# An attention kernel in which PE issues each odd step's scores before the pair's value products, instead of behind them

## The chip, the cores and the metric

One Trainium2 chip, one of its cores. The metric is the device time of one execution in microseconds. The engines are PE (matrix products and transposes), DVE (vector), ACT (scalar and activation), POOL (GpSimd) and SP (it issues DMA here). Each takes its own instructions in the order in which the program lists them, and semaphores tie the engines together.

## The reference

A block with eight sequences of 1024 tokens, 256 channels, all float32: a layer norm, then attention with eight query heads on one shared key and value head, and a channel-mixing network, both added to the input.

```
xn = layernorm(x)
q = xn @ Wq + bq (8 heads of 128) + pe;  k, v = split(xn @ Wkv + bkv);  k = k + pe
probs = softmax(causal(q k^T / sqrt(128)))
attn = (probs v) @ Wo
xr, xk = mu * xn + (1 - mu) * xn_shifted_by_one_token      (one mu for each)
ffn = sigmoid(xr Wr^T) * (square(relu(xk Wk^T)) Wv^T)
out = x + attn + ffn
```

## The kernel before

A batch row (one sequence) is worked off in 64 **steps**. A step is 16 tokens times 8 heads, so 128 query rows on the partitions, against the keys up to its own: its width is `width(s)`, from 16 columns (step 0) to 1024 (step 63). Two steps, 2p and 2p+1, are a **pair**; pairs share one product with the values. Every product in float32 accuracy is made of three passes of rounded halves (high times high, high times low, low times high), `PASSES` and `product`.

Each engine's program is a loop of **turns** (`turns()`); in turn `it` it does one stage of several steps at once:

- PE, `turn`: transposes of the probabilities of step it-6 into `pT` (L1139; from step 16 on only for odd steps); the "fillers" of the turn (L1036, L1081, L1091, L1123: projections `Q`, `KV`, feed-forward `FK`, `FR`, `FV`, the transposes `XT` and `KT`, and the output projection `WO`), as the tables `TURNS` and `WO_AT` place them; in odd turns from 9 on the value products of pair (it-9)/2 into the one bank `pO` (L1173 and, for the first pair of a row of tiles, L1181); last the scores of step `it` into `pS` (L1036), 3 products below step 32, 6 from there on.
- DVE, `turn`, in this order: reciprocal of the row sums, `rec` (L914), of step it-2; for even steps from 16 on the 32x32 transpose `Y` of step it-3; the low half of the transposed probabilities, `pt` (L940, L932); emptying the turn's fillers (`qtmp` L850, `xtok` L975 and others), norms and mixes; the low half of the value product, `ot` (L994); then the masked scores and their row bound, `X` and `bias` (L1015), of step `it`.
- ACT, `turn`: high halves `pt` (L688, L695), mixes, `qt` (L661); fillers' results, such as `xt` and `xnt` of XT (L637, L644); high half `ot` of the value product (L759); then the exponential of step it-1 (L766).
- POOL: the low halves of queries, mixes and of `pt` (L542), and the scaling of `X` by `rec`.
- SP: probabilities of even steps from 16 on travel to `park_dram` and back as `Z`.

Before the scores of step s PE waits on `masked` until DVE has read step s-2 out of the same bank pair `pS[s % 2]`. From step 32 on, where scores take both banks of a pair, all fillers but those with a place in `G_BANK` use the one bank `pG`, and a filler waits for what empties the filler before it (`wait_emptied`). The value products wait on `o_lo` (L994) of the pair before, on `t_hi`, `t_lo`, `turned_hi` and `turned_lo`. ACT's L759 waits on `pv_done`, DVE's L994 on `o_hi`, DVE's L1015 on `s_filled`.

Of the kernel before, what the change touches and what calls it, by code (L numbers as in the profile page):

```python
# [5 lines left out]
H, D = 8, 128  # L6
# [3 lines left out]
TPC = CHUNK // P  # L10
NC = T // CHUNK
NT = T // P
PAIRS = H // 2
SUB = P // H
STEPS = NT * H
# [12 lines left out]
PER = TPC * H  # L28
LAST_IT = STEPS + LEAD
SHARED = NT // 2 * H  # L30
# [77 lines left out]
def turned(s):  # L108

    return s >= 16 and s % 2 == 0  # L110
# [30 lines left out]
def width(s):  # L141
    return s // H * P + (s % H + 1) * SUB
# [73 lines left out]
BEFORE = users_before()  # L216


def build(nc, x_d, wq_d, wkv_d, wo_d, wr_d, wk_d, wv_d, bq_d, bkv_d, mu_d, pet_d, out_d, park_d):
# [6 lines left out]
    with ExitStack() as ctx:  # L226
        def sb(name, shape, dt=F):
            return ctx.enter_context(nc.sbuf_tensor(name, shape, dt))

        def pb(name, shape):  # L230
            return ctx.enter_context(nc.psum_tensor(name, shape, F))
# [8 lines left out]
        kt = [sb(f"kt{i}", [P, T], R) for i in range(2)]  # L240
# [8 lines left out]
        qt = [sb(f"qt{i}", [P, 2, CHUNK // SUB, H, SUB], R) for i in range(2)]  # L249
# [31 lines left out]
        pS = [pb(f"pS{i}", [P, 2, 512]) for i in range(2)]  # L281
# [31 lines left out]
        kt_ready = sem("kt_ready")  # L313
# [8 lines left out]
        q_ready = sem("q_ready")  # L322
        q_first = sem("q_first")
# [16 lines left out]
        s_filled = sem("s_filled")  # L340
        masked = sem("masked")
# [53 lines left out]
        def chunk_no(b, c):  # L395

            return 0 if b is None else b * NC + c
# [629 lines left out]
        def _(pe):  # L1027
            PASSES = ((0, 0), (0, 1), (1, 0))

            def product(out, terms, start=True, stop=True):  # L1030

                n = len(terms) * len(PASSES)
                k = 0
                for a, m in terms:
                    for i, j in PASSES:
                        last = nc.tensor.matmul(out, a[i], m[j], start=start and k == 0, stop=stop and k == n - 1)  # L1036
                        k += 1
                return last


            def wait_emptied(b, u):
                kind, c, p = u
                if kind == "S":
                    pe.wait_ge(masked, b * STEPS + c + 1)
                    return
                if kind == "T":
                    pe.wait_ge(t_lo, b * T_BODY + T_FIRST[c] + p + 1)
                    return
                n = chunk_no(b, c)
                if kind == "XT":  # L1050
                    pe.wait_ge(xnt_ready, n + 1)
                    if b is None:
                        pe.wait_ge(xt_ready, 1)
                elif kind == "KV":
                    pe.wait_ge(kv_ready, 2 * n + 2)
                elif kind == "KT":
                    pe.wait_ge(v_turned, n + 1)
                elif kind == "Q":
                    pe.wait_ge(q_sum, (n * PAIRS + p) * 2 + 2)
                elif kind == "FK":  # L1060
                    pe.wait_ge(relu_ready, n + 1)
                elif kind == "FR":
                    pe.wait_ge(tanh_ready, n + 1)
                elif kind == "FV":
                    pe.wait_ge(gated_ready, n + 1)
                else:
                    pe.wait_ge(out_ready, b * NT + c * TPC + p + 1)
# [59 lines left out]
            def turn(b, it):  # L1127
                first_row = b == 0
                s = it - T_LAG
                if 0 <= s < STEPS and not turned(s):  # L1130
                    pe.wait_ge(normed, b * N_BODY + N_FIRST[s + 1])
                    if scaled_by_act(s):
                        pe.wait_ge(scaled, b * C_FIRST[STEPS] + C_FIRST[s + 1])
                    for m, (k, nk) in enumerate(t_banks(s)):
                        u = T_FIRST[s] + m
                        if BEFORE[b, ("T", s, m)]:
                            wait_emptied(*BEFORE[b, ("T", s, m)])
                        for i in range(nk):
                            last = nc.tensor.transpose(pT[u % 2][:, i * P:(i + 1) * P],  # L1139
                                                       x_row(s, (k + i) * P, (k + i + 1) * P), ident[:, :])  # L1140
                        last.then_inc(t_filled, 1)
                for u in FILL[it]:
                    if u[0] == "WO":
                        fill(b, u)
                for u in FILL[it]:
                    if u[0] != "WO" and u != ("KT", NC, 0) and not absent(b, u[1]):
                        fill(b, u)
                part = it - PV_LAG
                if 0 <= part < STEPS:
                    pair = part // 2  # L1150
                    nk = part // H + 1
                    plain = nk - packed(2 * pair)
                    work = [(k, i, j) for i, j in ((0, 0), (1, 0), (0, 1)) for k in range(plain)]
                    early = len(work) // 2 if nk > 8 else 0
                    for n in range(early, len(work)) if part % 2 else range(early):
                        k, i, j = work[n]
                        if n == 0:
                            if pair % (PER // 2) == 0:
                                pe.wait_ge(v_ready, b * NC + part // PER + 1)
                            if pair or not first_row:  # L1160
                                pe.wait_ge(o_lo, b * (STEPS // 2) + pair)
                            for s in (2 * pair + 1, 2 * pair):
                                if turned(s):
                                    pe.wait_ge(turned_hi, turned_no(b, s) + 1)
                                else:
                                    pe.wait_ge(t_hi, b * T_BODY + T_FIRST[s + 1])
                        if n == 2 * plain:
                            for s in (2 * pair + 1, 2 * pair):
                                if turned(s):
                                    pe.wait_ge(turned_lo, turned_no(b, s) + 1)  # L1170
                                else:
                                    pe.wait_ge(t_lo, b * T_BODY + T_FIRST[s + 1])
                        last = nc.tensor.matmul(pO[:, 0:2 * P], v[i][:, k, :], pt[j][:, pair % 2, k, :],  # L1173
                                                start=n == 0, stop=n == 3 * nk - 1)
                    if part % 2:
                        if packed(2 * pair):
                            pe.wait_ge(vs_loaded, 48 * (b * NC + part // PER + 1))
                            for s in (2 * pair, 2 * pair + 1):
                                if s in WITHIN:
                                    pe.wait_ge(within_lo, within_no(b, s) + 1)  # L1180
                            last = nc.tensor.matmul(pO[:, 0:2 * P], vs[:, part // H % TPC, :],  # L1181
                                                    pt[0][:, pair % 2, nk - 1, :], start=False, stop=True)
                        last.then_inc(pv_done, 1)
                s = it
                if s < STEPS:
                    qi = s // H
                    c = qi // TPC
                    w = width(s)
                    n = chunk_no(b, c)
                    if s % PER == 0:  # L1190
                        pe.wait_ge(kt_ready, n + 1)
                        pe.wait_ge(q_ready, n * H + H)
                        if first_row and s == 0:
                            pe.wait_ge(q_first, PAIRS)
                    if s >= 2 or not first_row:
                        pe.wait_ge(masked, b * STEPS + s - 1)
                    if s >= SHARED and BEFORE[b, ("S", s, 0)][1][0] != "S":
                        wait_emptied(*BEFORE[b, ("S", s, 0)])
                    halves = 1 if qi < 4 else 2
                    wn = w // halves  # L1200
                    for a in range(halves):
                        last = product(pS[s % 2][:, a, 0:wn],
                                       [([q[:, c % 2, s % PER, :, :].rearrange("p h q -> p (h q)")
                                         for q in qt],
                                         [k[:, a * wn:(a + 1) * wn] for k in kt])])
                    last.then_inc(s_filled, 1)
                if ("KT", NC, 0) in FILL[it] and not absent(b, NC):
                    fill(b, ("KT", NC, 0))

# [67 lines left out]
```

## Time and profile before

| what | value |
|---|---|
| time, median of 3 runs | 1512.04 us (1511.46 to 1514.94) |
| span of the profiled execution | 1512.0 us |
| PE busy | 1484.7 us (98%), 11724 instructions |
| weight load (PEld) busy | 1448.2 us (96%) |
| DVE busy | 1262.6 us (84%) |
| POOL busy | 1153.7 us (76%) |
| ACT busy | 1052.6 us (70%) |
| granted TensorE clock | 9 in tenths in all 40 slices |

The profiled execution took 0.04 us less than the median of the runs, so its rows and the median are on one scale. A row of the timeline reads: start in us, duration in us, engine, line and operation, tile written <- tiles read, shape, count; in brackets the idle time of that engine before it and who ended it. PE's matmuls overlap, so that the next group's first start lies some 0.15 us ahead of the modelled end of the group before. A batch row takes about 185 us, and the eight repeat each other; the rows below are of the batch row that begins at about 750 us, unless said.

### The profile page before, as it was taken

The page shows a single profiled execution, that of the slowest core. Times are in us where ns is not written, and L with a number is a line of the kernel's source. Part 1 is how long each engine was busy: PE and PEld are TensorE (multiplying, and loading weights), DVE is VectorE, ACT ScalarE, POOL GpSimd, SP SyncE. Part 2 cuts the span into 40 slices and gives each one's busy share as a digit, 9 for nine tenths or more (in the row PEclk, how much of TensorE's full clock was granted, in tenths as well). Part 3 has the DMA queues.
Part 4 walks back from the last instruction along what each step waited for, and adds up shares of the span by engine and source line. Part 5 has one row for each costly group of instructions (what it writes and reads, how often), then busy time and mean ns, then how long its engine had stood idle before and what let it go on. Part 6 is the DMA issues. An engine that isn't in the chain of part 4 may idle for free.

```text
span 1512.0 us, 36188 instructions
## 1 busy us (share of the span) xinstructions
PE 1484.7 (98%) x11724; PEld 1448.2 (96%) x11724; DVE 1262.6 (84%) x3424; ACT 1052.6 (70%) x2531; POOL 1153.7 (76%) x1665
## 2 busy tenths in 40 slices
PE   7999999999999999999999999999999999999998
PEld 6999999999999999999999999999999999999998
DVE  7988869888698896988879888788887988879875
ACT  5777667776677766767677676767767776777764
POOL 6787777787777787877778777778777787778774
PEclk9999999999999999999999999999999999999999
DMA  4144422444224542344423444134441344413453
GB/s 129 44 126 135 132 87 67 116 141 141 74 69 119 146 137 60 86 120 139 128 58 96 120 137 136 43 100 122 137 139 38 105 130 138 138 29 101 127 153 105
DMA packets 225801, 164.39 MB, mean 109 GB/s; under 512 B 51792, under 2 KB 220880, under 8 KB 225616
## 3 DMA queue, kind: packets, MB, share of 16 engines
q1 hardware_dynamic: 224768, 161.69, 37.1%
q8 instruction: 96, 1.57, 0.4%
q14 instruction: 89, 0.73, 0.2%
q10 hardware_dynamic: 848, 0.40, 0.1%
HBM read 81.27 MB, written 77.59 MB: 105 GB/s over the span
## 4 chain that ended last, share of the span: by engine, by line
PE 75%; DVE 10%; DMA 7%; SPq 3%; issue 3%; ACT 1%; POOL 1%; DVEq 0%; ACTq 0%; POOLq 0%
PE pS L1036 26%; PE pO L1173 21%; PE pG L1036 12%; PE pG L1123 8%; PE pT L1139 7%; DMA park_dram<-Y 5%; SPq L455 3%; DVE X L1015 2%; DVE mix L861 1%; DMA Z<-park_dram 1%; DVE Y L924 1%; DVE pt L940 1%; DVE qtmp L850 1%; PE pS L1123 1%; DVE xn L810 1%
## 5 line engine op out<-in xcount | busy, mean ns | idle before, releaser
L766 ACT ACTIVATE X<-X,bias 128x16 f32<-128x16 f32 (+56 forms) x512 | 376.0, 734 | 156.3 <-DVE bias L1015 154.8
L1036 PE MATMUL pS<-kt,qt 128*128 128x288 f32 (+41 forms) x2304 | 462.2, 329 | 4.1 <-DVE kv L837 2.5
L1173 PE MATMUL pO<-pt,v 128*128 128x256 f32 x3288 | 435.4, 283 | 2.5 <-DVE ot L994 2.4
L1173 PEld LDWEIGHTS pO<-pt,v 128*128 128x128 f32 x3288 | 399.8, 189 | 3.6 <-DVE ot L994 3.4
L575 POOL TENSOR_SCALAR X<-X,rec 128x16 f32<-128x16 f32 (+56 forms) x512 | 373.6, 730 | 26.9 <-DVE rec L914 16.2
L1015 DVE CUSTOM_DVE_ANT_0 X<-pS,mask 128x16 f32<-128x16 f32 (+56 forms) x512 | 353.7, 691 | 40.8 <-PE pS L1036 33.9
L1036 PEld LDWEIGHTS pS<-kt,qt 128*128 128x128 f32 x2304 | 365.2, 189 | 16.8 <-issue 3.7
L542 POOL TENSOR_TENSOR pt<-Z,pt 128x256 fp32r<-128x256 f32 (+5 forms) x192 | 317.7, 1655 | 78.7 <-ACT pt L688 77.8
L527 POOL TENSOR_TENSOR qt<-qtmp,qt 128x256 fp32r<-128x256 f32 x252 | 194.5, 772 | 62.8 <-ACT qt L661 55.2
L940 DVE TENSOR_TENSOR pt<-pT,pt 128x512 fp32r<-128x512 f32 (+3 forms) x440 | 207.7, 493 | 37.9 <-ACT pt L695 37.1
L759 ACT CAST ot<-pO 128x256 fp32r<-128x256 f32 x256 | 95.9, 375 | 173.4 <-PE pO L1173 94.3
L695 ACT CAST pt<-pT 128x512 fp32r<-128x512 f32 (+3 forms) x448 | 189.6, 453 | 11.8 <-PE pT L1139 11.4
L1139 PE MATMUL pT<-ident,X 128*128 128x128 f32 x1248 | 190.1, 274 | 0.8 <-DVE pt L940 0.8
L924 DVE STREAM_TRANSPOSE Y<-X 128x384 f32<-128x384 f32 (+5 forms) x192 | 172.1, 896 | 6.2 <-POOL X L575 3.8
L994 DVE TENSOR_TENSOR ot<-pO,ot 128x256 fp32r<-128x256 f32 x256 | 106.6, 416 | 83.6 <-ACT ot L759 82.1
L1123 PE MATMUL pG<-wo,ot 128*128 128x256 f32 x1344 | 169.7, 282 | 1.3 <-DVE qtmp L850 0.7
L688 ACT CAST pt<-Z 128x384 fp32r<-128x384 f32 (+5 forms) x192 | 148.1, 771 | 31.1 <-DMA Z<-park_dram 30.0
L1123 PEld LDWEIGHTS pG<-wo,ot 128*128 128x128 f32 x1344 | 160.0, 189 | 3.0 <-DVE qtmp L850 2.3
L1139 PEld LDWEIGHTS pT<-ident,X 128*128 128x128 f32 x1248 | 150.6, 141 | 9.9 <-POOL X L575 0.7
L1036 PE MATMUL pG<-xt,wq 128*128 128x256 f32 x1116 | 148.8, 283 | 1.3 <-POOL xt L515 0.8
L1036 PEld LDWEIGHTS pG<-xt,wq 128*128 128x128 f32 x1116 | 141.6, 190 | 4.5 <-DVE xtok L975 2.3
L573 POOL MEMSET X<- 128x16 f32 (+5 forms) x336 | 48.0, 143 | 105.1 <-DVE rec L914 104.5
(118 smaller groups left out, 1943.4 us busy)
## 6 DMA issues: line engine op xcount, KB each, us to landing
park_dram<-Y SPq DMA_DIRECT2D x32, 512.0 KB, 2.6
Z<-park_dram SPq DMA_DIRECT2D x128, 128.0 KB, 3.0
park_dram<-Y SPq DMA_DIRECT2D x32, 448.0 KB, 3.2
Z<-park_dram SPq DMA_DIRECT2D x128, 112.0 KB, 2.7
park_dram<-Y SPq DMA_DIRECT2D x32, 384.0 KB, 2.9
Z<-park_dram SPq DMA_DIRECT2D x128, 96.0 KB, 2.5
park_dram<-Y SPq DMA_DIRECT2D x32, 320.0 KB, 2.9
Z<-park_dram SPq DMA_DIRECT2D x128, 80.0 KB, 2.2
```

What stands on the lines that cost most here:

```text
L527: nc.gpsimd.tensor_tensor(qt[1][:, slot, :, h, :], qtmp[:, p % QTMP, i, :].rearrange("p (t q) -> p t q", q=SUB), qt[0][:, slot, :, h, :].b ...
L542: nc.gpsimd.tensor_tensor(pt_of(1, s)[:, 0:whole, :].rearrange("p k (a c) -> p a k c", a=4), Z[:, k % 2, :, 0:whole, :], pt_of(0, s)[:, 0: ...
L575: nc.gpsimd.tensor_scalar(x_row(s, 0, w), x_row(s, 0, w), rec[:, j:j + 1], 1.0, ALU.mult, ALU.mult).then_inc(normed, 1)
L695: nc.scalar.copy(pt_of(0, s)[:, k:k + nk, :], pT[u % 2][:, 0:nk * P].rearrange("p (k n) -> p k n", n=P)).then_inc(t_hi, 1)
L766: nc.scalar.activation(x_row(s, 0, w), x_row(s, 0, w), ACT.Exp, bias=bias[:, j:j + 1], scale=-1.0, accum_out=total[:, j:j + 1]).then_inc(e ...
L924: nc.vector.transpose(Y[:, k % 2, :, 0:nk, :].rearrange("p a k c -> p k a c"), x_row(s, 0, nk * P).rearrange("p (k a c) -> p k a c", a=4, ...
L940: low = nc.vector.tensor_tensor(pt_of(1, s)[:, k:k + whole, :], pT[u % 2][:, 0:whole * P].rearrange("p (k n) -> p k n", n=P), pt_of(0, s)[ ...
L1015: nc.vector.tensor_tensor_reduce(out=o, in0=scores, in1=m, scale=SCALE, scalar=HUGE, op0=ALU.add, op1=ALU.min, accum_out=bias[:, j:j + 1]) ...
L1036: last = nc.tensor.matmul(out, a[i], m[j], start=start and k == 0, stop=stop and k == n - 1)
L1123: last = nc.tensor.matmul(out[:, 0:E], ot[i][:, h, :], wo[j][:, h, :], start=(i, j, h) == (0, 0, 0), stop=i == 1 and h == H - 1)
L1139: last = nc.tensor.transpose(pT[u % 2][:, i * P:(i + 1) * P], x_row(s, (k + i) * P, (k + i + 1) * P), ident[:, :])
L1173: last = nc.tensor.matmul(pO[:, 0:2 * P], v[i][:, k, :], pt[j][:, pair % 2, k, :], start=n == 0, stop=n == 3 * nk - 1)
```

## The change

In PE's `turn` the block that issues the scores of step `it` stands ahead of the block that issues the value products, where it stood behind it. Both keep their waits. In even turns, in turns below 9 and in turns from 64 on (which carry the last value products of one batch row beside the first steps of the next) only one of the two blocks has anything to do, and nothing moves. The orders of DVE, ACT, POOL and SP are row for row the same.

```diff
@@ turn(b, it) of PE, behind the fillers @@
+                s = it
+                if s < STEPS:
...
+                    if s >= 2 or not first_row:
+                        pe.wait_ge(masked, b * STEPS + s - 1)
+                    if s >= SHARED and BEFORE[b, ("S", s, 0)][1][0] != "S":
+                        wait_emptied(*BEFORE[b, ("S", s, 0)])
...
+                    last.then_inc(s_filled, 1)
                 part = it - PV_LAG
                 if 0 <= part < STEPS:
...
                         last.then_inc(pv_done, 1)
-                s = it
-                if s < STEPS:
...
-                    last.then_inc(s_filled, 1)
                 if ("KT", NC, 0) in FILL[it] and not absent(b, NC):
                     fill(b, ("KT", NC, 0))
```

PE's order in turns 17 to 19 (the width in a pS<-kt,qt row names the step: 288 is step 17, 304 step 18, 320 step 19; L1196 and L1204 are the lines 1173 and 1181 after the change):

```order
-L1173 MATMUL pO<-pt,v 128x256 x3
-L1181 MATMUL pO<-pt,vs 128x256
 L1036 MATMUL pS<-kt,qt 128x288 x3
+L1196 MATMUL pO<-pt,v 128x256 x3
+L1204 MATMUL pO<-pt,vs 128x256
 L1139 MATMUL pT<-ident,X 128x128 x2
 L1036 MATMUL pS<-kt,qt 128x304 x3
 L1139 MATMUL pT<-ident,X 128x128 x2
 L1081 MATMUL pS<-ident,xn 128x128 x4
-L1173 MATMUL pO<-pt,v 128x256 x6
 L1036 MATMUL pS<-kt,qt 128x320 x3
+L1196 MATMUL pO<-pt,v 128x256 x6
```

The scores of steps 17 and 19 now start where the value products started.

PE's order in turns 39 to 41 (each of the 6 products of a step from 32 on has half its width; 320 is step 39, 328 step 40; pG<-wr,mh, pG<-xt,wq and pG<-wo,ot are the fillers FR, Q and WO, all in bank pG):

```order
 L1036 MATMUL pG<-wr,mh 128x256 x12
-L1173 MATMUL pO<-pt,v 128x256 x12
 L1036 MATMUL pS<-kt,qt 128x320 x6
+L1196 MATMUL pO<-pt,v 128x256 x12
 L1036 MATMUL pG<-xt,wq 128x256 x12
 L1036 MATMUL pS<-kt,qt 128x328 x6
 L1139 MATMUL pT<-ident,X 128x128 x5
 L1123 MATMUL pG<-wo,ot 128x256 x24
```

The value products of turn 39 now end right ahead of turn 40's Q.

PE's order in turns 51 to 53 (416 is step 51, 424 step 52; pG<-ident,xn is the filler XT, pG<-wr,mh the filler FR):

```order
-L1173 MATMUL pO<-pt,v 128x256 x18
 L1036 MATMUL pS<-kt,qt 128x416 x6
+L1196 MATMUL pO<-pt,v 128x256 x18
 L1081 MATMUL pG<-ident,xn 128x128 x4
 L1036 MATMUL pS<-kt,qt 128x424 x6
 L1139 MATMUL pT<-ident,X 128x128 x6
 L1036 MATMUL pG<-wr,mh 128x256 x12
```

The value products of turn 51 now stand between the scores and XT.

## Rows read from the trace of the kernel before

**Rows 1.** The page, busy time of each engine.

```profile
PE 1484.7 (98%) x11724; PEld 1448.2 (96%) x11724; DVE 1262.6 (84%) x3424; ACT 1052.6 (70%) x2531; POOL 1153.7 (76%) x1665
```

**Rows 2.** Waits, whole span: us in total, times, longest us.

```profile
PE pG L1081 <- DVE xtok L975: 4.1, 8, 0.6
PE pG L1036 <- POOL mh L533: 2.8, 7, 0.9
PE pS L1036 <- DVE kv L837: 2.5, 7, 1.3
ACT kt L649 <- PE pS L1036: 20.6, 7, 2.9
DVE ot L994 <- ACT ot L759: 82.1, 73, 3.5
```

**Rows 3.** Timeline, batch row from about 1120 us: a release of PE by POOL.

```profile
1196.07 1.76 POOL L533 TENSOR_TENSOR mh<-mix,mh 128x512 fp32r<-128x512 f32 x1
1197.98 1.65 PE L1036 MATMUL pG<-mh,wk 128*128 128x256 f32 x12 [0.30 <-POOL mh L533]
```

**Rows 4.** Timeline, turns 17 to 19.

```profile
795.36 0.28 PE L1181 MATMUL pO<-pt,vs 128*128 128x256 f32 x1
795.48 0.56 PE L1036 MATMUL pS<-kt,qt 128*128 128x288 f32 x3
795.68 0.37 ACT L759 CAST ot<-pO 128x256 fp32r<-128x256 f32 x1 [0.64 <-PE pO L1181]
796.08 0.42 DVE L994 TENSOR_TENSOR ot<-pO,ot 128x256 fp32r<-128x256 f32 x1 [0.37 <-ACT ot L759]
796.42 0.45 DVE L1015 CUSTOM_DVE_ANT_0 X<-pS,mask 128x288 f32<-128x288 f32 x1
797.10 0.96 PE L1173 MATMUL pO<-pt,v 128*128 128x256 f32 x6
```

**Rows 5.** Timeline, turns 39 to 41.

```profile
849.47 0.43 DVE L994 TENSOR_TENSOR ot<-pO,ot 128x256 fp32r<-128x256 f32 x1 [0.96 <-ACT ot L759]
849.97 0.82 DVE L1015 CUSTOM_DVE_ANT_0 X<-pS,mask 128x640 f32<-128x640 f32 x1
...
851.74 0.88 DVE L850 SCALAR_TENSOR_TENSOR qtmp<-pG,bq,pet 128x256 f32<-128x256 f32 x2
...
852.67 3.09 PE L1123 MATMUL pG<-wo,ot 128*128 128x256 f32 x24
```

**Rows 6.** Timeline, turns 43 to 45.

```profile
864.36 1.14 PE L1036 MATMUL pS<-kt,qt 128*128 128x352 f32 x6
...
865.69 0.89 DVE L1015 CUSTOM_DVE_ANT_0 X<-pS,mask 128x704 f32<-128x704 f32 x1 [0.30 <-PE pS L1036]
...
867.01 1.19 PE L1173 MATMUL pO<-pt,v 128*128 128x256 f32 x8
```

**Rows 7.** Timeline, turns 49 to 53.

```profile
885.10 0.99 DVE L1015 CUSTOM_DVE_ANT_0 X<-pS,mask 128x800 f32<-128x800 f32 x1 [0.41 <-PE pS L1036]
...
886.42 2.37 PE L1173 MATMUL pO<-pt,v 128*128 128x256 f32 x18
...
888.62 1.31 PE L1036 MATMUL pS<-kt,qt 128*128 128x416 f32 x6
888.82 0.37 ACT L759 CAST ot<-pO 128x256 fp32r<-128x256 f32 x1 [0.16 <-PE pO L1173]
...
890.40 0.59 ACT L637 CAST xt<-pG 128x512 fp32r<-128x512 f32 x1 [0.24 <-PE pG L1081]
890.89 0.60 ACT L644 COPY xnt<-pG 128x512 f32<-128x512 f32 x1
...
891.94 1.66 PE L1036 MATMUL pG<-wr,mh 128*128 128x256 f32 x12
```

**Rows 8.** Timeline, turns 57 to 59.

```profile
914.73 1.12 DVE L1015 CUSTOM_DVE_ANT_0 X<-pS,mask 128x928 f32<-128x928 f32 x1 [0.58 <-PE pS L1036]
...
916.35 2.72 PE L1173 MATMUL pO<-pt,v 128*128 128x256 f32 x21
```

More of the change, by code:

```diff
@@ L1147, in turn @@
                         fill(b, u)
+                s = it
+                if s < STEPS:
+                    qi = s // H
+                    c = qi // TPC
+                    w = width(s)
+                    n = chunk_no(b, c)
+                    if s % PER == 0:
+                        pe.wait_ge(kt_ready, n + 1)
+                        pe.wait_ge(q_ready, n * H + H)
+                        if first_row and s == 0:
+                            pe.wait_ge(q_first, PAIRS)
+                    if s >= 2 or not first_row:
+                        pe.wait_ge(masked, b * STEPS + s - 1)
+                    if s >= SHARED and BEFORE[b, ("S", s, 0)][1][0] != "S":
+                        wait_emptied(*BEFORE[b, ("S", s, 0)])
+                    halves = 1 if qi < 4 else 2
+                    wn = w // halves
+                    for a in range(halves):
+                        last = product(pS[s % 2][:, a, 0:wn],
+                                       [([q[:, c % 2, s % PER, :, :].rearrange("p h q -> p (h q)")
+                                         for q in qt],
+                                         [k[:, a * wn:(a + 1) * wn] for k in kt])])
+                    last.then_inc(s_filled, 1)
                 part = it - PV_LAG
@@ L1183, in turn @@
                         last.then_inc(pv_done, 1)
-                s = it
-                if s < STEPS:
[L1186 to L1205, printed above, removed]
-                    last.then_inc(s_filled, 1)
                 if ("KT", NC, 0) in FILL[it] and not absent(b, NC):
```

## The prediction

> **What bounds the kernel now.** I read the page's busy times first, then PE's waits, then the timeline of one batch row, turn by turn. PE is busy 98% of the span, its weight loads 96% [rows 1]. In the list of waits the longest of PE's own are three that add to 9.4 us in 1512 [rows 2]. So PE's stream of work sets the time: the other engines count only where they make it stall. The change takes no work from PE and gives it none: the same products stand in another order, and the span can only move by stalls that come or go. The stalls that could go are few (the 9.4 us and some shorter ones). So the question is how much slack each wait of PE has in the new order.
>
> **What moves.** 28 odd turns of each batch row (9 to 63), 224 in all, change. Within each, the scores start where the value products started, and the value products end where the scores ended. At the turn's end nothing has moved. Two edges change.
>
> (a) The scores of step s ask earlier, by the length of the value products (0.96 us at step 19, 2.72 at step 59 [rows 4, 8]), whether DVE has read step s-2.
>
> (b) The value products end later, by the length of the scores (0.56 us at step 17, 1.31 at step 51 [rows 4, 7]). Behind them ACT's L759 waits, and behind that, on ACT, the exponential of step s-1 and all of turn s+1. DVE's L994 waits for L759, and behind L994, on DVE, stands L1015 of this very step s. The scores lie ready earlier, but DVE does not reach them earlier, since L994 is ahead of them.
>
> **How much later L1015 ends.** Before, where DVE had caught up, L759 and L994 ran beside the scores, and L1015 started right behind the scores: at 865.69 with the scores from 864.36 for 1.14 us, 0.19 us after their end [rows 6]. Now the turn ends with the value products. From that end on, as in [rows 4]: 0.04 us from the end of L1181 (795.36 + 0.28 = 795.64) to L759 at 795.68, 0.37 for L759, 0.03 to L994 at 796.08, 0.42 for L994, and L1015 starts at 796.42, 0.08 before L994's end. That is 0.04 + 0.37 + 0.03 + 0.42 - 0.08 = 0.78 us after the turn's end instead of 0.19, so **0.6 us later**. Where DVE was behind anyway and L994 waited for nothing, it is 0.1 or nothing. L994 waited in 73 of 256 cases [rows 2]; of the 28 changed turns of the batch row from 750 us I get some 0.6 in 8, 0.4 in one (17), 0.2 to 0.35 in 5, and about 0.1 or less in 14, by the same sum on each.
>
> **Where PE meets that.** PE restarts some 0.15 us after a release: POOL's L533 ends at 1196.07 + 1.76 = 1197.83 and PE starts at 1197.98 [rows 3]. A stall is then the delay, less the slack, plus 0.15.
>
> 1. Turn 19: L1015 of step 17 ended at 796.87, the scores of step 19 will want to start at 797.10, slack 0.23. In turn 17 the scores end at 796.04; L759, L994, L1015 behind that put L1015's end at 796.04 + 0.78 + 0.45 = 797.27, 0.40 later [rows 4]. Stall 0.40 - 0.23 + 0.15 = **0.32**.
> 2. Turn 45: L1015 of step 43 ended at 866.58, the new start is 867.01, slack 0.43 [rows 6]. Stall 0.6 - 0.43 + 0.15 = **0.32**.
> 3. Turn 51: 885.10 + 0.99 = 886.09 against 886.42, slack 0.33 [rows 7]. Stall **0.42**.
> 4. Turn 59: 915.85 against 916.35, slack 0.50 [rows 8]. Stall **0.25**.
> 5. Turn 41, filler WO in the one bank pG: it starts at 852.67, 0.05 after DVE's L850 has emptied Q out of that bank (851.74 + 0.88 = 852.62). From L994 at 849.47 on DVE runs L1015, L914, L932 and L850 with no pause over 0.1 us, and L994 had waited 0.96 us for ACT, so DVE had no backlog at its start. The 0.6 us of step 39 go through whole [rows 5]. Stall **0.60**. Filler Q of turn 38 before FR of turn 39 is the same case with 0.4 us of idle DVE in between: about **0.1**.
> 6. Turn 53, filler FR: it waits for ACT's L644, which empties XT. ACT's L759 of turn 51 moves from 888.82 to the end of the turn, 888.62 + 1.31 + 0.04 = 889.97, by 1.15. The exponential stands behind it, then L637, which had 0.24 us of idle time before it. So L644 ends at 891.49 + 1.15 - 0.24 = 892.40, and FR can start at 892.55 instead of 891.94 [rows 7]. Stall 0.61; I take **0.55**, since the stall of turn 51 does not shift ACT and PE against each other but some of the gap may be shorter in other batch rows.
>
> The next smallest slacks of the scores, 0.3 at step 29 and 0.5 to 0.6 at steps 21 and 23, meet delays of 0.1 and cost nothing or a tenth. Between the places DVE and ACT wait for PE again, so a stall does not pay for the next one, and they add: 0.32 + 0.32 + 0.42 + 0.25 + 0.60 + 0.10 = 2.01 us in 8 batch rows, 16.1 us; 0.55 us in 7 of them (the last has no next chunk to prepare), 3.9 us. **Sum 20.0 us.** The profiled span of 1512.0 stands 0.04 under the median: 1512.0 + 20.0 = **1532 us**.
>
> **What it gives back.** The value products ask later for their inputs, but PE stalls ahead of them almost nowhere in the odd turns 9 to 63, so nothing is won there. In turn 63 ACT's L649 waits for the scores of step 63, 20.6 us in 7 waits [rows 2]; these now come some 2.5 us earlier each. Yet PE does not stall behind it in turn 64, so it is ACT's idle time alone. The three stalls of [rows 2] hang on POOL, and on DVE work that stands ahead of L994 in its turn; neither moves. I put the gain at 0, bounded by 2 us.
>
> **A rule weighed.** What the timeline shows of bank pO in turn 17 is that L759 and L994 empty it while PE works in pS and pT, and in the new order they would do so while PE works on the next turn [rows 4]. The Trainium skill (page "Perfetto Trace Analysis", section "Optimizing Tensor Performance") says that independent groups of products should rotate through banks, so that the emptying of one overlaps the next. Both orders follow it, and by it alone the time would be unchanged. It is the first rival.
>
> **Rivals.**
>
> *The cover suffices* (unchanged, 1512 to 1516 us). For it: two steps stand between a score and the next use of its bank, and the emptying of pO lies beside other products in either order. Against it: the slacks of 0.23 to 0.50 us and the 0.05 us at WO, which are smaller than 0.6. It would need L1015 to come at most 0.2 us later. Chance 0.09.
>
> *Only the scores' own waits count* (about 1521 us). If DVE and ACT make up their delay before the fillers' turns (points 5 and 6), 0.32 + 0.32 + 0.42 + 0.25 = 1.3 us times 8 is left, 10.5 us, and less without the release step: 6.6 to 10.5, so 1519 to 1523. Chance 0.14.
>
> *The delay travels further* (1541 to 1560 us). The exponential of an even step comes 0.8 to 1.3 us later in turns 33 to 61. It is what POOL's scaling, the transposes on DVE and the trip through park_dram wait for; a late trip holds ACT's L688, and all of ACT behind it. If one more stall of 0.6 us comes in five more turns of each batch row, that is 24 us more, 1556. Against it: these have two or more turns of slack. Chance 0.07.
>
> *Faster* (about 1503 us). If ACT's 2.9 us of turn 63 and the earlier scores let DVE run ahead, the stalls of [rows 2] in the following chunks, 9.4 us, would go. It decides whether DVE and ACT enter the next batch row earlier and keep that lead for 32 turns; but they wait for PE in most of them, and what is waited for there does not come earlier. Chance 0.04.
>
> **Numbers.** Chance of my forecast, stalls at both kinds of place (1523 to 1541): 0.66. The range 1518 to 1541 takes in the second rival and leaves out the first, the last two: 0.8 inside. A measurement of this kernel tells about 0.3% (4.5 us) from no change. Faster by more than that 0.04, within it 0.09, slower by more 0.87.
>
> **What would show it.** In the changed kernel's waits: PE pS L1036 behind DVE bias L1015 about 24 to 32 times, some 8 us with the exposed weight loads; PE pG L1123 behind DVE qtmp L850 at every turn 41, up by 0.6 each; PE pG L1036 behind ACT xnt L644, 7 times; ACT kt L649 behind PE nearly gone; DVE ot L994 behind ACT ot L759 well above the 82.1 us of before [rows 2], since DVE then waits for the turn's end. It is wrong if PE shows no new wait in turns 19, 45 and 51, or if the value products of odd turns had in truth been held by something that a later start relieves.

## The result, and the profile after

The changed kernel took 1532.49 us (median of 4 runs, 1531.55 to 1533.2) against 1511.9 us before: ratio 1.0127, 95% interval 1.0114 to 1.0139. It is slower by 20.6 us; forecast were 1532 us and 20.0 us. The profiled execution has a span of 1530.9 us against 1512.0, 18.9 us more. Span and time are not one scale, although the section on the profile before took them for one: in every run that has both, the span (first to last instruction) is 1.7 to 2.9 us shorter than the time. So the profile of before, 1512.0 us, can only be of the slowest of its four runs, 1514.94 us, and what the tables below give as growth is measured from that one.

The page, span and busy times, after:

```profile
span 1530.9 us, 36188 instructions
...
PE 1498.3 (98%) x11724; PEld 1452.8 (95%) x11724; DVE 1259.6 (82%) x3424; ACT 1052.4 (69%) x2531; POOL 1149.1 (75%) x1665
```

It answers to [rows 1]. The counts are the same, and DVE, ACT and POOL did their work in the same time to 5 us. PE's "busy" grew by 13.6 us although it has no instruction more: its matmuls overlap, and part of a short stall hides inside the modelled length of the matmul ahead of it. At the filler WO of turn 41 below, the idle time is 0.47 us in the row of the weight load (PEld) and 0.23 us in that of the matmul. So the stalls are looked for in the weight loads.

Waits, whole span, of after (us in total, times, longest us); in these kernels L1196 and L1204 are the value products:

```profile
PEld pS L1036 <- DVE bias L1015: 8.4, 36, 0.5
PEld pG L1123 <- DVE qtmp L850: 4.9, 9, 0.7
PEld pG L1036 <- ACT xnt L644: 2.6, 7, 0.4
DVE ot L994 <- ACT ot L759: 133.3, 109, 3.5
ACT kt L649 <- PE pS L1036: 2.4, 7, 0.4
```

The same view of before, the rows that answer to the first two (there was none for the third):

```profile
PEld pS L1036 <- DVE bias L1015: 0.6, 1, 0.6
PEld pG L1123 <- DVE qtmp L850: 2.3, 7, 0.5
```

The scores' wait for L1015 came once and now comes 36 times: at steps 19, 45, 51 and 59 in all eight batch rows, and at four other steps once (the view leaves out waits up to 0.15 us). The filler behind ACT's L644 waits in 7 of them. DVE's wait for L759 rose from 82.1 to 133.3 us, and ACT's L649 hardly waits any more, both against [rows 2].

Timeline of after, turns 17 to 19 (it answers to [rows 4]; 128x288 is step 17, 128x320 step 19):

```profile
804.56 0.56 PE L1036 MATMUL pS<-kt,qt 128*128 128x288 f32 x3
...
805.31 0.28 PE L1204 MATMUL pO<-pt,vs 128*128 128x256 f32 x1
...
805.63 0.37 ACT L759 CAST ot<-pO 128x256 fp32r<-128x256 f32 x1 [0.71 <-PE pO L1204]
...
806.04 0.42 DVE L994 TENSOR_TENSOR ot<-pO,ot 128x256 fp32r<-128x256 f32 x1 [0.73 <-ACT ot L759]
...
806.38 0.45 DVE L1015 CUSTOM_DVE_ANT_0 X<-pS,mask 128x288 f32<-128x288 f32 x1
...
806.89 0.44 PEld L1036 LDWEIGHTS pS<-kt,qt 128*128 128x128 f32 x3 [0.24 <-DVE bias L1015]
```

The scores of step 17 end at 805.12 and lie there until L1015 takes them at 806.38, since the value products (to 805.59), L759 and L994 stand ahead of it. L1015 ends at 806.83 and PE goes on at 806.89 with the scores of step 19, 0.06 us later: PE's weight load had been idle for 0.24 us.

Timeline of after, turns 39 to 41 ([rows 5]), 49 to 51 and 51 to 53 ([rows 7]):

```profile
860.05 0.42 DVE L994 TENSOR_TENSOR ot<-pO,ot 128x256 fp32r<-128x256 f32 x1 [1.52 <-ACT ot L759]
860.40 0.81 DVE L1015 CUSTOM_DVE_ANT_0 X<-pS,mask 128x640 f32<-128x640 f32 x1
...
861.33 0.42 DVE L932 TENSOR_TENSOR pt<-Z,pt 32x128 fp32r<-32x128 f32 x1
...
861.78 0.87 DVE L850 SCALAR_TENSOR_TENSOR qtmp<-pG,bq,pet 128x256 f32<-128x256 f32 x2
...
862.71 0.65 PEld L1123 LDWEIGHTS pG<-wo,ot 128*128 128x128 f32 x5 [0.47 <-DVE qtmp L850]
```

```profile
895.76 0.98 DVE L1015 CUSTOM_DVE_ANT_0 X<-pS,mask 128x800 f32<-128x800 f32 x1
...
896.80 0.49 PEld L1036 LDWEIGHTS pS<-kt,qt 128*128 128x128 f32 x3 [0.31 <-DVE bias L1015]
```

```profile
900.37 0.37 ACT L759 CAST ot<-pO 128x256 fp32r<-128x256 f32 x1 [1.05 <-PE pO L1196]
...
900.64 0.98 ACT L766 ACTIVATE X<-X,bias 128x816 f32<-128x816 f32 x1
...
901.61 0.57 ACT L637 CAST xt<-pG 128x512 fp32r<-128x512 f32 x1
...
902.08 0.59 ACT L644 COPY xnt<-pG 128x512 f32<-128x512 f32 x1
...
902.73 0.66 PEld L1036 LDWEIGHTS pG<-wr,mh 128*128 128x128 f32 x5 [0.38 <-ACT xnt L644]
```

In each of the three the chain runs with no pause over 0.1 us from the end of the value products to the instruction on which PE waits. Turn 39's own filler, FR, starts 1.32 us after the scores of step 38 in before and in after: no wait came there.

**Where the time sits.** I took the starts of the scores of every even step from the trace (their places in the program are the same in all kernels) and added, over batch rows 1 to 7 (of 0 to 7), how much longer each stretch of steps became. "Ends" is step 62 to step 0 of the next row, for the seven such ends. Batch row 0 and the first and last microseconds are not in the table; in after they hold 3.7 of the 18.9 us. Each row is one profiled execution, which need not lie at the median of its kernel: that of e1 took 1518.33 us against a median of 1523.09, that of e7 1514.87 against 1519.45.

| kernel | 0 to 16 | 16 to 22 | 22 to 36 | 36 to 48 | 48 to 62 | ends |
|---|---|---|---|---|---|---|
| after | 0.9 | 1.9 | 2.0 | 2.7 | 6.8 | 0.9 |
| after, again (e12) | 1.4 | 1.8 | 5.8 | 1.8 | 7.1 | 0.7 |
| e1, turns 1 mod 4 | 1.5 | -0.2 | 2.1 | -1.9 | 0.4 | 1.9 |
| e2, turns 3 mod 4 | 0.4 | -1.0 | -0.1 | 1.1 | 3.0 | 0.1 |
| e3, all but five turns | 1.5 | -0.2 | 3.8 | -1.5 | 0.8 | 1.9 |
| e4, late L759 alone | 0.0 | 0.0 | 2.0 | 1.8 | 4.3 | 2.7 |
| e5, swap on DVE | 2.9 | -0.3 | 1.8 | 0.0 | 3.1 | 0.2 |
| e6, swap on ACT | 1.5 | 3.2 | 3.5 | 2.3 | 5.2 | 0.4 |
| e7, both swaps | 0.8 | -0.3 | 0.6 | -2.1 | 0.7 | 0.2 |
| e8, before with both swaps | 3.6 | 0.2 | 3.0 | -1.3 | 0.7 | 0.3 |
| e9, turns from 36 on | 0.2 | 0.0 | -0.3 | 2.7 | 7.2 | 0.6 |
| e10, turns below 36 | 0.9 | 1.9 | 3.7 | 0.8 | 0.2 | 0.0 |
| e11, swaps in 37 to 47 | -0.1 | 0.0 | 1.6 | -1.3 | -1.2 | 0.0 |

How far such a number can be trusted shows where nothing was changed. The stretch 16 to 22 repeats to 0.1 us where PE's order in it is the same (e4, e9, e11 against before; after against e12 and e10). The stretch 22 to 36 does not: one batch row took 36.1 to 40.6 us there, e11 has 1.6 us more although nothing moved in it, and after has 2.0 in one execution and 5.8 in another.

**Pace without a wait.** Some pairs of turns change length although no engine is waited for. The starts of value products and fillers of one group lie 113 to 114 ns apart or 117 to 118, and the new order swaps the one for the other in some turns. The 15 value products of turn 47 went from 118 to 113, and that pair of turns became 0.11 us shorter; the 21 of turn 61 went from 113 to 118, and its pair became 0.12 longer. This repeats in every execution with the new order there (after, e12, e7, e9) and is absent in e4 and e10, where these turns are as before. What sets the pace no run shows.

### The profile page after: what moved, and what is told of

The parts are those of the page before. It is cut to its first block, busy times and chain, and to the rows that moved or that the text cites. A ratio compares the mean times of both kernels' runs of the same rounds, so it can differ in the third digit from the quotient of the medians.

```text
span 1530.9 us, 36188 instructions
## 1 busy us (share of the span) xinstructions
PE 1498.3 (98%) x11724; PEld 1452.8 (95%) x11724; DVE 1259.6 (82%) x3424; ACT 1052.4 (69%) x2531; POOL 1149.1 (75%) x1665
## 4 chain that ended last, share of the span: by engine, by line
PE 74%; DVE 9%; DMA 7%; issue 3%; SPq 3%; ACT 2%; POOL 2%; DVEq 0%; ACTq 0%; POOLq 0%
PE pS L1036 24%; PE pO L1196 21%; PE pG L1036 12%; PE pG L1123 9%; PE pT L1139 6%; DMA park_dram<-Y 5%; SPq L455 3%; DVE X L1015 2%; DMA Z<-park_dram 1%; DVE mix L861 1%; DVE pt L940 1%; DVE Y L924 1%; ACT ot L759 1%; DVE qtmp L850 1%; POOL X L575 1%
## 5 line engine op out<-in xcount | busy, mean ns | idle before, releaser
L1036 PE MATMUL pS<-kt,qt 128*128 128x288 f32 (+41 forms) x2304 | 475.5, 333 | 5.0 <-DVE kv L837 2.7
L766 ACT ACTIVATE X<-X,bias 128x16 f32<-128x16 f32 (+56 forms) x512 | 375.1, 733 | 111.8 <-DVE bias L1015 110.1
L1196 PE MATMUL pO<-pt,v 128*128 128x256 f32 x3288 | 426.7, 280 | 2.7 <-DVE ot L994 2.5
L1196 PEld LDWEIGHTS pO<-pt,v 128*128 128x128 f32 x3288 | 410.0, 188 | 7.6 <-DVE ot L994 3.6
L1015 DVE CUSTOM_DVE_ANT_0 X<-pS,mask 128x16 f32<-128x16 f32 (+56 forms) x512 | 352.6, 689 | 12.1 <-PE pS L1036 7.5
L759 ACT CAST ot<-pO 128x256 fp32r<-128x256 f32 x256 | 95.6, 373 | 282.1 <-PE pO L1196 178.3
L994 DVE TENSOR_TENSOR ot<-pO,ot 128x256 fp32r<-128x256 f32 x256 | 107.5, 420 | 136.4 <-ACT ot L759 133.3
L924 DVE STREAM_TRANSPOSE Y<-X 128x384 f32<-128x384 f32 (+5 forms) x192 | 172.3, 898 | 6.7 <-POOL X L575 4.2
L688 ACT CAST pt<-Z 128x384 fp32r<-128x384 f32 (+5 forms) x192 | 148.0, 771 | 23.0 <-DMA Z<-park_dram 21.9
L1036 PEld LDWEIGHTS pG<-xt,wq 128*128 128x128 f32 x1116 | 138.3, 190 | 3.0 <-DVE xtok L975 1.5
```

The lines of the kernel that those rows point to most:

```text
L766: nc.scalar.activation(x_row(s, 0, w), x_row(s, 0, w), ACT.Exp, bias=bias[:, j:j + 1], scale=-1.0, accum_out=total[:, j:j + 1]).then_inc(e ...
L924: nc.vector.transpose(Y[:, k % 2, :, 0:nk, :].rearrange("p a k c -> p k a c"), x_row(s, 0, nk * P).rearrange("p (k a c) -> p k a c", a=4, ...
L1015: nc.vector.tensor_tensor_reduce(out=o, in0=scores, in1=m, scale=SCALE, scalar=HUGE, op0=ALU.add, op1=ALU.min, accum_out=bias[:, j:j + 1]) ...
```

## The experiments

The three theories: the cost is a handful of stalls, each from two changed turns or one chain on DVE or ACT (mine); it is spread evenly over the changed turns; it comes from the lateness of ACT's L759 alone. In all diffs `scores()` and `values()` are the two blocks of PE's turn.

**e1, e2: every other changed turn.**

```
-                (value products, then scores)
+                for stage in (scores, values) if it % 4 == 1 else (values, scores):     # e1;  it % 4 == 3 in e2
+                    stage()
```

> The scores go first only in turns 9, 13, 17, ... 61 (turn mod 4 = 1), the value products first in the others. My theory: the cost sits in a few turns. Four of them (19, 45, 51, 59) need two changed turns in a row, the earlier one to make L1015 late and the later one to ask early; here no two neighbours are changed, so they cost nothing. The fillers of turns 41 and 53 hang on turns 39 and 51, which are not changed. Only FR of turn 39 behind turn 37 is left, 0.05 us: 1512 to 1514 us. Rival, a cost spread evenly over the changed turns (20.6 us over 28 of them a batch row, 14 changed here): 1522 us.

> The scores go first only in turns 11, 15, 19, ... 63 (turn mod 4 = 3). My theory: again no two neighbours are changed, so no stall on masked; but turns 39 and 51 are changed, so WO of turn 41 waits on L850 (0.3 to 0.4 us in 8 batch rows) and FR of turn 53 on L644 (0.45 in 7): 5.5 to 6.5 us, 1517 to 1519 us. PE pG L1036 behind ACT xnt L644 shows 7 times. Rival, a cost spread evenly: 1522 us, as for the other half.

e1: ratio 1.0051 (1.0036 to 1.0067), 1523.09 us against 1515.49. e2: 1.0028 (1.0015 to 1.0042), 1519.91 us. By the times e1 is a miss: 7.6 us where 0 to 2 were expected, near the 10 us of an even spread. The waits tell the halves apart. e1, then e2:

```profile
PEld pS L1036 <- DVE bias L1015: 1.2, 2, 0.7
```

```profile
PEld pS L1036 <- DVE bias L1015: 0.5, 1, 0.5
...
PEld pG L1036 <- ACT xnt L644: 2.7, 7, 0.4
```

The 36 waits for L1015 need two changed neighbours: either half alone has one or two. The 7 waits for L644 come with turn 51, in e2. e2 cost 4.4 us, somewhat under the 5.5 to 6.5 expected; its 1519.91 us is over the 1517 to 1519 only because before took 1515.49 here. In the table it has its cost where it was expected (36 to 62: 4.1 us). e1 has none there (-1.5), and 5.5 us at 0 to 16, 22 to 36 and the batch rows' ends, of which I had expected nothing; since its profiled execution is one of its fastest, a part of its 7.6 us is in no table at all. The two halves together cost 12.0 us of 20.6. The 8.6 that are missing need changed neighbours, and the waits at steps 19, 45, 51 and 59, which come in neither half, are 0.24, 0.21, 0.31 and 0.15 us in after, 7.3 us over eight batch rows.

e1's ends (1.9 us) have a cause that the trace shows. Turn 57 of e1, timeline:

```profile
916.77 0.43 DVE L994 TENSOR_TENSOR ot<-pO,ot 128x256 fp32r<-128x256 f32 x1 [3.33 <-ACT ot L759]
917.11 1.11 DVE L1015 CUSTOM_DVE_ANT_0 X<-pS,mask 128x928 f32<-128x928 f32 x1
```

Counted from the start of step 58's scores, L1015 of step 57 ended at 1.47 us before [rows 8] and at 2.06 in e1. From there DVE has only one pause over 0.1 us, the same 0.12 us before L924 as in before, until L850 of turn 62, which ends at 16.82 instead of 16.27. FV of turn 63 starts 0.06 us behind it. In after it is the same to 0.03 us (2.06 and 16.82), and in e2, where turn 57 is not changed, DVE pauses for 0.56 us at turn 59 and L850 ends at 16.28. So the delay enters at turn 57, and it reaches FV whether turn 59 is changed (after) or not (e1, e3).

**e3: all changed turns but five.** The condition is `it not in (19, 39, 45, 51, 59)`.

> The scores go first in all odd turns but 19, 39, 45, 51 and 59. My theory: 23 of 28 turns stay changed and the named stalls go: what is left are the small terms (0.05 to 0.1 at turns 39 and 61, 0.1 at the batch rows' ends): 1513 to 1516 us. Rival, spread evenly: 23/28 of 20.6 us, 1529 us.

1521.02 us, 1.0039 (1.0024 to 1.0054): 5.5 us. 23 of 28 turns are changed and 15 us of 20.6 are gone, so an even spread (1529) is out. The five turns hold 4.2 us in the stretch 36 to 48 and 6.0 in 48 to 62, over 7 batch rows. The upper end of what I expected, 1516, is missed by 5 us; again 0 to 16, 22 to 36 and the ends (turn 57 is changed here) hold it.

**e4: L759 late, PE's order untouched.**

```
                     act.wait_ge(pv_done, b * (STEPS // 2) + pair + 1)
+                    if it < STEPS:
+                        act.wait_ge(s_filled, b * STEPS + it + 1)
```

> PE's order is that of before. ACT's L759 of turn s waits, besides, for the scores of step s, so it starts as late as in the changed kernel, and L994 and L1015 behind it. My theory: this is edge (b) without edge (a): L1015 is 0.6 us late, but the scores ask later again by the length of the value products, so the stalls on masked are gone and those on the fillers of turns 41 and 53 stay: 5.5 to 6.5 us, 1517 to 1519 us. Rival, that lateness of L759 alone is the whole cost: 1531 us. Second rival, that PE's order itself costs (the order of its instructions, not the waits): 1512 us.

1530.29 us, 1.0097 (1.0082 to 1.0112): 14.8 us where I expected 5.5 to 6.5. The direct waits are gone as expected, since the scores ask later again:

```profile
PEld pS L1038 <- DVE bias L1017: 0.5, 1, 0.5
PEld pG L1125 <- DVE qtmp L852: 4.9, 9, 1.0
PEld pG L1038 <- ACT xnt L644: 3.0, 7, 0.4
PEld pG L1038 <- DVE qtmp L852: 2.4, 7, 0.3
```

The second and third are turns 41 and 53, in the size of after (4.9 and 2.6). The fourth I had not foreseen. It is FV of turn 63, behind L850 (here L852) of turn 62. Timeline of e4, turns 61 to 63:

```profile
940.53 0.85 DVE L852 SCALAR_TENSOR_TENSOR qtmp<-pG,bq,pet 128x256 f32<-128x256 f32 x2
...
941.44 1.65 PE L1038 MATMUL pG<-wv,kh 128*128 128x256 f32 x12
```

and the same place before:

```profile
929.80 0.85 DVE L850 SCALAR_TENSOR_TENSOR qtmp<-pG,bq,pet 128x256 f32<-128x256 f32 x2
...
930.99 1.62 PE L1036 MATMUL pG<-wv,kh 128*128 128x256 f32 x12
```

Before, FV started 0.34 us after L850's end (930.65); now 0.06 us after it (941.38). L994 waited for nothing in turn 61 in either kernel: DVE was behind, and L850's delay of 0.62 us is that of turn 57 (L1015 ends at 2.10 instead of 1.47 there), carried through five turns of DVE work. With that the ends of the batch rows cost 0.4 us each (2.7 in the table), and the pair around turn 57 0.25. The stretch 22 to 36 and the first and last microseconds, which vary anyway, hold the rest. By the medians the lateness alone costs about three quarters of the change (14.8 of 20.6 us), and the earlier question of the scores adds the waits for L1015. "L759 alone" (1531) is nearly met by the time, but not by the waits.

**e5, e6, e7: the changed kernel with DVE's or ACT's order swapped.** In e5 L1015 stands ahead of L994, in e6 the exponential L766 ahead of L759, in e7 both.

```
 (DVE, end of turn)                       (ACT, end of turn)
-    o_hi wait, L994: ot low              -    pv_done wait, L759: ot high
     s_filled wait, L1015: masked              masked wait, L766: exponential of it - 1
+    o_hi wait, L994: ot low              +    pv_done wait, L759: ot high
```

> The changed kernel, and on DVE the masked scores (L1015) stand ahead of the low half of the value product (L994) in the turn. My theory: L1015 then starts right behind the scores and no longer behind the value products; the stalls on masked and the one on L850 (turn 41) go, the one on ACT's L644 (turn 53, 0.45 us in 7 batch rows) stays: 1514 to 1517 us. Rival, that the delay comes through ACT (L759 and the exponential behind it): still 1529 to 1532 us.

> The changed kernel, and on ACT the exponential of step s-1 (L766) stands ahead of the high half of the value product (L759). My theory: only the stall of turn 53 (0.45 us in 7 batch rows) hangs on the exponential behind L759; the rest hangs on DVE's order: 1526 to 1530 us. Rival, delay through ACT: 1514 to 1517 us.

> The changed kernel with both swaps. My theory: all five named stalls go, and DVE and ACT have their work ahead of the wait for the value products: 1508 to 1513 us. Rival, that something else of PE's new order costs: over 1516 us.

e5: 1525.76 us, 1.0081 (1.0057 to 1.0105). e6: 1531.57, 1.0119 (1.0103 to 1.0134). e7: 1519.45, 1.0041 (1.0026 to 1.0055), beside 1514.83 for before. The waits of e5, e6 and e7 in this order (L1007 is the masked scores where DVE's order is swapped):

```profile
PEld pG L1123 <- DVE qtmp L850: 2.9, 7, 0.6
PEld pG L1036 <- ACT xnt L644: 2.7, 7, 0.4
...
PEld pS L1036 <- DVE bias L1007: 0.9, 2, 0.5
```

```profile
PEld pS L1036 <- DVE bias L1015: 9.6, 40, 0.7
PEld pG L1123 <- DVE qtmp L850: 6.0, 9, 1.2
```

```profile
PEld pG L1123 <- DVE qtmp L850: 1.5, 4, 0.5
...
PEld pS L1036 <- DVE bias L1007: 0.5, 1, 0.5
```

DVE's swap takes away the waits for L1015 (36 to 2) and leaves L644's 7; ACT's takes away L644's 7 and leaves L1015's (40); both take away both. These two kinds of stall hang each on the in-order queue to which it was put down, and e6 shows that ACT's lateness is not what the scores wait for.

Turn 41 does not fit that. I had expected its stall to go in e5, since DVE then takes the scores first. It did not: the pair of turns around it grew by 0.29 us in after, 0.29 in e5, 0.27 in e6 and 0.05 in e7 (mean of batch rows 1 to 6). In e5 DVE has a new pause on its way to L850, in all eight batch rows:

```profile
856.83 0.16 DVE L914 RECIPROCAL rec<-total 128x1 f32<-128x1 f32 x1 [0.38 <-ACT X L766]
```

ACT's exponential still stands behind the late L759, and L914 needs its row sum. So L850 is late through DVE's queue in after and e6 and through ACT's in e5, and only both swaps free it.

The times of e6 (1526 to 1530 expected) and e7 (1508 to 1513) are over their ranges by 2 and 6 us, e5's (1514 to 1517) by 9; before itself took 1514.83 us on this chip instead of 1511.9. e7 is also over the 1516 us that I had named for the rival, a cost of PE's new order itself; e8 weighs that. For e5 and e6 the table shows part of the excess at 0 to 16 and 22 to 36.

**e8: the kernel before with both swaps.**

> The kernel before with both swaps, as a control of what the swaps do in the old order of PE. My theory: L1015 has to wait for the scores and L994 behind it comes up to 1 us later, which nobody waits for; the exponential comes earlier: 1508 to 1514 us, within 0.3% of before. Were it slower than before by as much as the changed kernel, then the swaps and not the stalls would be what the comparison shows.

1521.02 us, 1.0044 (1.0029 to 1.006): 6.2 us slower than before, where I expected no difference. The table has it at 0 to 16 (3.6) and 22 to 36 (3.0), in no place of the named stalls (36 to 48 is 1.3 shorter). So by the medians PE's new order costs nothing on the whole once both swaps are in (e7 1.0041, e8 1.0044), and the swaps by themselves cost some 6 us in e8. That e7 pays for them in the same places isn't shown: its one profile is of its fastest execution and has next to nothing there. One part is seen in e8. With the swap L994 (here L1016) of turn 63 stands behind L1015 of step 63, and the value products of turn 65 wait for it, since it empties pO: the stretch from step 0 to 2 is 0.5 us longer in e8 in batch rows 1 to 6. The waits of e8:

```profile
PEld pO L1173 <- DVE ot L1016: 7.3, 12, 1.5
```

Before had 4 such waits, 3.4 us together.

**e9, e10, e12: the two halves, and the changed kernel again, on one chip.** The condition for the new order is `it >= 36` in e9, `it < 36` in e10.

> The scores go first in turns 37 to 63 only. My theory: of the named stalls the ones of turns 41, 45, 51, 53 and 59 stay, and the carried delay at FV of turn 63; turn 19's goes. By the trace of the changed kernel the stretches from turn 36 on, the batch rows' ends and the tail held 12 to 13 us of 19 us: span 1524 to 1526 us, ratio to before 1.008 to 1.009. Rival, spread evenly over the turns (14 of 28): half of 1.27%, 1.0064.

> The scores go first in turns 9 to 35 only, the other half. My theory: turn 19's stall (0.23 us in 8 batch rows) and small ones: 4 to 7 us, ratio 1.003 to 1.005; this and the late half add up to the changed kernel's within 0.2%. Rival, spread evenly: 1.0064. If the two halves add to clearly less or more, the stalls are not independent of each other.

> The changed kernel again, on the chip and beside the runs of before that the other three are compared with: ratio 1.011 to 1.014.

e9: 1529.7 us, 1.0082 (1.006 to 1.0104). e10: 1522.97, 1.0046 (1.0029 to 1.0064). e12: 1536.54, 1.0128 (1.0108 to 1.0147), beside 1516.57 for before. The halves add to 1.0128, as much as e12, so within some 0.3% their costs add. Every run of e9 is slower than every run of e10, so the late half costs more, 13.1 us against 6.4, though each interval taken alone just reaches the even share of 1.0064. The prediction had put 17.4 us into the late half and 2.6 into the early one; most of the 6.4 us of the early half is not in its terms. The span of e9, 1528.3 us, is over the 1524 to 1526 expected, 1.6 us of it by the slow end told of in the last section. The waits for L1015 split 26 and 10:

```profile
PEld pS L1036 <- DVE bias L1015: 6.0, 26, 0.5
```

```profile
PEld pS L1036 <- DVE bias L1015: 2.7, 10, 0.5
```

**e11: new order and both swaps in turns 37 to 47 alone.** All three `for stage in` lines carry the condition `36 <= it < 48`.

> The scores first on PE, L1015 ahead of L994 on DVE and the exponential ahead of L759 on ACT, all three in turns 37 to 47 only; the rest is the kernel before. My theory: this stretch was 2.1 us shorter over 7 batch rows with everything swapped, since DVE's work up to L850 is done earlier and PE waits less at WO of turn 41: span 1509 to 1511 us, ratio 0.998 to 1.000. If the swaps bring stalls wherever they are, it is over 1.003.

1514.29 us against 1516.57, 0.9982 (0.9968 to 0.9995). PE's weight load waits less for L850, 1.2 us in 3 cases instead of 2.3 in 7:

```profile
PEld pG L1131 <- DVE qtmp L854: 1.2, 3, 0.6
```

It is the only version faster than before, by 0.18%, under what I had named as the least that a measurement tells; the interval excludes no change by a hair. Its span, 1514.0, is above the 1509 to 1511 that I expected (on this chip before has no profile of its own beside it); 1.6 us of it are the slow end told of in the last section. The gain is not mainly the wait that I had named: the pairs of turns from 42 to 50 are 0.06 to 0.14 us shorter each, with no wait of PE in before there, and that is the pace of its matmuls.

## Why the prediction was right

**PE sets the time, the order alone moves nothing.** Right on the whole, not in each place: PE's counts are the same, and in e7, with PE's new order and the waits out of its way, steps 36 to 62 take 1.5 us less than before over seven batch rows. But that is a balance of pairs that became 0.1 us shorter (43, 45, 47, 49) and longer (61) by the pace of the matmuls alone, which the prediction had at nothing.

**Edges (a) and (b), and L1015 0.6 us late.** Right. In turn 49 L1015 ended 1.18 us after the turn's end before and 1.76 after, in turn 17 0.83 and 1.23.

**The named stalls.** Six of the seven were there, each behind the instruction named; the one at FR of turn 39 was not. Their sizes, as the growth of the pair of turns around each (mean of batch rows 1 to 6) and as the growth of the idle time of PE's weight load at the place itself:

| place | forecast us | pair grew by us | wait grew by us |
|---|---|---|---|
| turn 19 | 0.32 | 0.23 | 0.24 |
| turn 39 (FR) | 0.10 | 0.05 | none |
| turn 41 (WO) | 0.60 | 0.29 | 0.34 |
| turn 45 | 0.32 | 0.23 | 0.21 |
| turn 51 | 0.42 | 0.34 | 0.31 |
| turn 53 (FR) | 0.55 | 0.45 | 0.38 |
| turn 59 | 0.25 | 0.07 | 0.15 |
| sum | 2.56 | 1.66 | 1.63 |

So the sum of the named terms, 20.0 us, measured about 12.7, and the forecast came out right to 0.6 us because costs that it did not have made up for it. That the two are the same size is luck. What was sized wrong:

First, the step from a release to PE's next start. I took 0.15 us from a filler behind POOL [rows 3]; for the scores behind L1015 it is 0.06 us (806.83 to 806.89), in all eight batch rows, and the same for FR behind L644 (902.67 to 902.73). My own rows had it for a release by DVE: 0.05 us at WO [rows 5]. This is the 0.08 to 0.11 us by which the waits of turns 19, 45, 51 and 59 fell short, and most of turn 53's. At turn 41 L850 was late by the 0.6 us forecast in six of eight batch rows, but for what L932 ahead of it took more or less: 0.41 to 0.98 us before and 0.42 to 0.67 after, on the mean of batch rows 1 to 6 0.19 us less.

Second, backlog that is carried. I worked out L1015's delay of each turn from that turn alone, put turn 61 at 0.1 or less, and said that between the places DVE waits for PE again, so that the stalls add. But for the 0.12 us that it had before as well, DVE does not wait between turns 57 and 62, so turn 57's delay goes through to FV of turn 63. The pairs around 59 and 61 and the ends of the batch rows grew by some 0.3 us a batch row together, 0.29 in e1 and 0.31 in after. Since turn 59's stall is in after and not in e1, it does not add to the rest: without it PE waits that much longer at FV. The pair around turn 57 grew by another 0.09.

What is left is not explained by a named wait: 0.3 to 0.8 us a batch row in the stretch 22 to 36, where how much of it is the change cannot be said from single executions (after, e10 and e12 had 2.0, 3.7 and 5.8 us over 7 batch rows), 0.9 us at 0 to 16, and batch row 0 with the start and end of the program.

**"What it gives back: nothing".** Right for the waits: ACT's wait before L649 fell from 20.6 to 2.4 us and no PE stall went with it. The pace gave back 0.05, 0.11 and 0.09 us in the pairs around turns 43, 47 and 49, 2 us over eight batch rows, which is the bound that I had set.

**The rivals.** "The cover suffices" fell with the measured time, and with it the rule of the Trainium skill ("Perfetto Trace Analysis", "Optimizing Tensor Performance") as a forecast of no change: the banks do rotate in both orders, and PE stalled all the same, by 0.24 us in turn 19, since what it waited for stood in a queue behind the emptying. "Only the scores' own waits count" fell with L644's 7 waits. "Travels further" was priced far too high; the carried backlog is of its kind, in a place where I had not looked. "Faster" had nothing for it.

## What to carry to other kernels

When two blocks change places on the engine that sets the time, ask of each other engine in which order it takes their results. Here the scores came earlier and were taken later, because the consumer's queue had the other block's result first; the same swap in the consumers' queues (e7) took every named stall away, to 0.05 us. Work out the slack of each wait from the trace, and carry a delay on through every stretch in which the delayed engine has no pause, not only to the end of its turn: here it came through five turns. Two late queues can hide behind each other, as at turn 41, where mending one showed the other.

## What the runs showed that I had not expected

The clock of PE at the very end. The last pair's value products (24 matmuls) wait for the trip through memory. Windows of before (us, PE busy, PEld, DVE, ACT, POOL, granted clock, DMA share, GB/s), then of e4:

```profile
1500.00:1503.00 3.00, 0.93 (x8) 0.73 (x8) 1.62 (x3) 1.69 (x4) 2.35 (x1) 1.00 0.00 0
1503.00:1506.00 3.00, 2.64 (x24) 2.44 (x22) 0.00 (x0) 0.33 (x1) 0.00 (x0) 1.00 0.00 0
```

```profile
1514.00:1517.00 3.00, 0.53 (x5) 0.32 (x3) 1.62 (x3) 2.07 (x4) 2.10 (x1) 0.91 0.00 0
1517.00:1521.00 4.00, 3.99 (x23) 3.99 (x24) 0.00 (x0) 0.00 (x0) 0.25 (x1) 0.64 0.00 0
```

Ahead of these matmuls PE had been idle for 2.07 us in before and 2.48 in e4. The granted clock stayed at 1.00, the level of 2.4 GHz, in before and was 0.64 of it on the mean of four microseconds in e4, part of them at 1.2 GHz. The same 24 matmuls took 3.02 us in before and 4.37 in e4. It came in five of the fourteen profiled executions (e2, e4, e9, e10, e11: 4.4 to 4.6 us for the 24), behind idle times of 1.95 to 2.48 us, and did not come in nine others behind 1.08 to 2.59 us, so the length of the pause does not tell the two apart. These 1.4 to 1.6 us at the end of a run say nothing on the change.

The second is how far executions of one kernel differ within turns 22 to 36: 36.1 to 40.6 us for a batch row, up to 4 us in one row, and before itself at 1511.9, 1515.49, 1514.83 and 1516.57 us on the occasions on which it was timed. For batch row 5, the longest of them, the traces show one cause, the trip of the probabilities through park_dram. Rows of before, then of e10:

```profile
1011.40 0.62 ACT L688 CAST pt<-Z 128x512 fp32r<-128x512 f32 x1 [2.22 <-DMA Z<-park_dram]
```

```profile
1018.86 0.62 ACT L688 CAST pt<-Z 128x512 fp32r<-128x512 f32 x1 [2.98 <-DMA Z<-park_dram]
...
1022.18 1.12 PEld L1036 LDWEIGHTS pS<-kt,qt 128*128 128x128 f32 x6 [2.22 <-DVE kt L832]
```

Behind L688 on ACT stands L649, L832 on DVE needs that, and the scores of step 32 need L832: their weight load waited 1.50 us in before and 2.22 in e10. In e1 ACT waited there 0.78 us and the weight load 0.34, and the pair of turns ahead of these scores was 1.67 us shorter than in before. In e11, where nothing ahead of turn 37 was moved, they were 2.61 and 1.84 us, so the wait differs without the change. No experiment took it away; what makes the trip long stays open, as does the rest of the cost of some 5 us in the early turns that e1, e3 and e8 share.
